# Bucket sums of both batches behind the second scores, and first products that wait for each part of their input

## The reference

```python
def causal_linear_attn(q, k, v):
    q = jax.nn.softmax(q, axis=-1)
    k = jax.nn.elu(k) + 1.0
    bq, bk, bv = (z.reshape(b, h, u, BUCKET, e) for z in (q, k, v))   # BUCKET 64, 4 buckets of 256 tokens
    k_cum = jnp.cumsum(bk.sum(axis=-2), axis=-2)
    ctx = jnp.einsum('bhund,bhune->bhude', bk, bv)
    ctx = jnp.cumsum(ctx, axis=2)
    ctx = ctx / (k_cum[..., None] + 1e-06)
    ctx = jnp.pad(ctx, ((0, 0), (0, 0), (1, 0), (0, 0), (0, 0)))[:, :, :-1]
    return jnp.einsum('bhund,bhude->bhune', bq, ctx)
...
for i in range(DEPTH):                                                # DEPTH 4
    x = x + self_attention(layer_norm(x, ln1_g[i], ln1_b[i]), Wq[i], Wk[i], Wv[i], Wo[i], bo[i])
    h = layer_norm(x, ln2_g[i], ln2_b[i])
    x = x + (jax.nn.gelu(h @ W1[i] + b1[i], approximate=False) @ W2[i] + b2[i])
```

## Time and profile before

| | |
|---|---|
| median of 3 runs | 1082.23 us (1082.07 to 1083.27) |
| the profiled execution | 1085.59 us, span 1083.8 us |
| busy in the span | PE 1000.8 us, PEld 845.2, DVE 680.7, ACT 560.8, POOL 483.0 |
| one step in the middle (409.92 to 456.79) | 46.87 us |

### The profile page before, as it was taken

The page is one execution under the profiler, slowest core; times in us unless marked ns, Lnnn a source line. Parts: engine busy times, 40 slices in busy tenths (PEclk is TensorE's granted clock), DMA queues, the critical chain, the costliest instruction groups (busy, mean ns, idle before and its releaser), DMA issues.

```text
span 1083.8 us, 22544 instructions
## 1 busy us (share of the span) xinstructions
PE 1000.8 (92%) x8461; PEld 845.2 (78%) x8461; DVE 680.7 (63%) x1502; ACT 560.8 (52%) x1338; POOL 483.0 (45%) x378
## 2 busy tenths in 40 slices
PE   3577999999999999999999999999999979999997
PEld 3455888888878878886887888788888758987887
DVE  2556576666857676776767667676341776657543
ACT  1416665756656574765657476665715333435210
POOL 7215446526843652585365358633416220006441
PEclk9777999999999999999999999999999999999999
DMA  5201000000300000021000102001036464640001
GB/s 186 79 1 39 2 2 16 2 16 2 98 24 2 16 2 16 2 79 42 2 15 2 16 2 79 2 2 45 2 95 165 123 157 98 143 112 1 20 20 40
DMA packets 71547, 47.72 MB, mean 44 GB/s; under 512 B 44463, under 2 KB 68111, under 8 KB 71439
## 3 DMA queue, kind: packets, MB, share of 16 engines
q1 hardware_dynamic: 71439, 46.27, 15.6%
HBM read 44.16 MB, written 2.10 MB: 43 GB/s over the span
## 4 chain that ended last, share of the span: by engine, by line
PE 65%; DVE 10%; ACT 8%; SPq 7%; issue 6%; POOL 2%; DMA 1%; POOLq 0%; DVEq 0%; ACTq 0%
PE A L1099 17%; PE F L1099 16%; PE F L1220 13%; ACT prob L920 5%; PE A L1465 4%; PE A L1130 3%; SPq L298 2%; PE A L1169 2%; DVE smax L582 2%; DVE xt L519 2%; PE A L1186 2%; PE A L1125 2%; SPq L306 1%; SPq L308 1%; PE A L1438 1%
## 5 line engine op out<-in xcount | busy, mean ns | idle before, releaser
L1099 PE MATMUL F<-xt,w 128*128 128x512 f32 x960 | 244.5, 405 | 8.3 <-ACT scratch L1082 3.9
L1099 PEld LDWEIGHTS F<-xt,w 128*128 128x128 f32 x960 | 176.1, 190 | 56.2 <-DVE xt L519 7.7
L385 POOL TENSOR_TENSOR ht<-scratch,ht 128x512 fp32r<-128x512 f32 x128 | 175.0, 1386 | 46.0 <-ACT ht L952 44.9
L1220 PEld LDWEIGHTS F<-w,ht 128*128 128x128 f32 x1536 | 182.8, 188 | 11.8 <-issue 9.3
L1220 PE MATMUL F<-w,ht 128*128 128x256 f32 x1536 | 189.3, 282 | 1.9 <-POOL ht L385 1.9
L374 POOL TENSOR_TENSOR rstd<-var,minus_half 128x4 f32<-128x4 f32 x32 | 38.0, 1187 | 242.5 <-DVE var L501 242.5
L949 ACT ACTIVATE scratch<-F,b_now 128x512 f32<-128x512 f32 x128 | 87.6, 685 | 43.1 <-PE F L1099 22.1
L1099 PE MATMUL A<-wa,xt 128*128 128x512 f32 x384 | 96.5, 409 | 3.8 <-issue 3.6
L1099 PEld LDWEIGHTS A<-wa,xt 128*128 128x128 f32 x384 | 74.2, 196 | 21.6 <-issue 3.9
L380 POOL TENSOR_TENSOR x<-x,vec_f 128x1024 f32<-128x1024 f32 x16 | 37.9, 2368 | 105.5 <-DVE scratch L514 105.5
L952 ACT ACTIVATE ht<-scratch 128x512 fp32r<-128x512 f32 x128 | 80.9, 632 | 4.1
(11 more groups left out here) (200 smaller groups left out, 1960.2 us busy)
## 6 DMA issues: line engine op xcount, KB each, us to landing
raw_f<-in_L_attn_W_dram SPq DMA_DIRECT2D x8, 1024.0 KB, 5.5
scratch<-in_L_ffn_fc_B_dram SPq DMA_DIRECT2D x32, 256.0 KB, 3.5
scratch<-in_L_ffn_fc_A_dram SPq DMA_DIRECT2D x32, 256.0 KB, 3.5
x<-in_x_dram SPq DMA_DIRECT2D x4, 512.0 KB, 7.4
raw_f<-in_L_ffn_fc_A_dram SPq DMA_DIRECT2D x32, 64.0 KB, 2.3
scratch<-in_x_dram SPq DMA_DIRECT2D x1, 2048.0 KB, 9.4
raw_f<-in_L_ffn_fc_B_dram SPq DMA_DIRECT2D x32, 64.0 KB, 3.0
out_dram<-x SPq DMA_DIRECT2D x3, 512.0 KB, 2.9
```

Source lines behind the costliest of these rows:

```text
L385: pool.tensor_tensor(ht[:, 1, m, :], hf[:, m % 2, :], ht[:, 0, m, :].bitcast(F32), ALU.subtract).then_inc(h_lo, 1)
L1099: last = pe.matmul(out, lhs(a, c), rhs(b, c), start=k == 0, stop=k == len(total) - 1)
L1220: last = pe.matmul(F[:, t % 2, 0:D], ht[:, a, c, P * t:P * t + P], w2[:, b, c, :], start=k == 0, stop=k == len(passes) - 1)
```

## The change

Three things change. `pe_ctx` makes the sums of both batches in one go, in banks 0 and 1 for batches 0 and 1, with the 128-token pieces of both batches first; it stands behind `pe_s(1)` and in front of `y(3)`. The wait for ACT's copy of the query transposes (`qnt_out`) moves from `pe_s(1)` to the sums. `dve_ctx` handles both batches with one set of three operations, behind the minimum of the second batch. And a new `first_product`, used by `pe_h(0)` and `pe_qk(0)`, waits for the low half of chunk 0, then for the high half of chunk 1 in front of the fourth matmul, and for the low half of chunk 1 in front of the sixth.

```diff
-        def dve_ctx(dve, n, b):
+        def dve_ctx(dve, n):
...
-            dve.wait_ge(ctx_psum, 2 * n + b + 1)
-            ps = A[:, 1 - b, 0:3 * HB].rearrange("p (j e) -> p j e", j=3)
-            dve.tensor_scalar(kcum[:, b, :], ps[:, :, E], 1e-6, None, ALU.add).then_inc(kcum_done, 1)
+            dve.wait_ge(ctx_psum, n + 1)
+            ps = A[:, 0:2, 0:3 * HB].rearrange("p b (j e) -> p b j e", j=3)
+            dve.tensor_scalar(kcum[:, :, :], ps[:, :, :, E], 1e-6, None, ALU.add).then_inc(kcum_done, 1)
...
                 if attn:
-                    dve_ctx(dve, n, 0)
                     dve_max(dve, n, 1)
+                    dve_ctx(dve, n)
                 y_add(3)
                 if attn:
-                    dve_ctx(dve, n, 1)
                     dve_prec(dve, n)
...
+        def first_product(pe, out, lhs, rhs, i, n):
+
+            total = [(c, a, b) for c in range(DC) for a, b in PASSES]
+            for k, (c, a, b) in enumerate(total):
+                if k == 0:
+                    pe.wait_ge(xt_lo[i], 2 * n + 1)
+                elif (a, b) == (0, 0):
+                    pe.wait_ge(xt_hi[i], 2 * n + c + 1)
+                elif b == 1 and c == 1:
+                    pe.wait_ge(xt_lo[i], 2 * n + c + 1)
+                last = pe.matmul(out, lhs(a, c), rhs(b, c), start=k == 0, stop=k == len(total) - 1)
+            return last
...
             if i == 0:
-                pe.wait_ge(xt_lo[0], 2 * n + 2)
                 pe.wait_ge(wa_ready, l + 1)
+                first_product(pe, A[:, QK_BANKS[i], :], lambda a, c: wa[:, a, c, P * i:P * i + P],
+                              lambda b, c: xt[0][:, b, c, :], 0, n).then_inc(qk_psum, 1)
+                return
...
                 pe.wait_ge(exp_done, 2 * n + 1)
-                pe.wait_ge(qnt_out, n + 1)
...
-        def pe_ctx(pe, n, b):
-
-            def part(j, t, rows, start, stop):
+        def pe_ctx(pe, n):
+
+            def part(b, j, t, rows, start, stop):
                 for h in range(NH):
-                    last = pe.matmul(A[E * h:E * h + E, 1 - b, j * HB:(j + 1) * HB], kexp[0:rows, t, E * h:E * h + E],
+                    last = pe.matmul(A[E * h:E * h + E, b, j * HB:(j + 1) * HB], kexp[0:rows, t, E * h:E * h + E],
                                      v8[0:rows, t, NH + h, :], start=start, stop=stop, skip_group_check=True)
                 return last
-            part(0, 2 * b, BUCKET, True, False)
-            part(2, 2 * b + 1, BUCKET, False, False)
-            part(2, 2 * b, P, False, False)
-            part(1, 2 * b, P, False, True).then_inc(ctx_psum, 1)
+            for b in range(2):
+                part(b, 2, 2 * b, P, True, False)
+                part(b, 1, 2 * b, P, False, False)
+            for b in range(2):
+                part(b, 0, 2 * b, BUCKET, False, False)
+                last = part(b, 2, 2 * b + 1, BUCKET, False, True)
+            last.then_inc(ctx_psum, 1)
...
                     pe_qnt(pe, n)
-                    pe_ctx(pe, n, 0)
                     pe_s(pe, n, 1)
+                    pe.wait_ge(qnt_out, n + 1)
+                    pe_ctx(pe, n)
                     y(3)
-                    pe_ctx(pe, n, 1)
```

More of the change, by code:

```diff
@@ L556, in dve_features2 @@
                               ALU.mult).then_inc(qn_done, 1)
-        def dve_ctx(dve, n, b):
-            dve.wait_ge(ctx_psum, 2 * n + b + 1)
-            ps = A[:, 1 - b, 0:3 * HB].rearrange("p (j e) -> p j e", j=3)
-            dve.tensor_scalar(kcum[:, b, :], ps[:, :, E], 1e-6, None, ALU.add).then_inc(kcum_done, 1)
[L563 to L567, removed]
+        def dve_ctx(dve, n):
+            dve.wait_ge(ctx_psum, n + 1)
+            ps = A[:, 0:2, 0:3 * HB].rearrange("p b (j e) -> p b j e", j=3)
+            dve.tensor_scalar(kcum[:, :, :], ps[:, :, :, E], 1e-6, None, ALU.add).then_inc(kcum_done, 1)
+            dve.wait_ge(kcum_done, n + 1)
+            dve.reciprocal(kcum[:, :, :], kcum[:, :, :]).then_inc(krec_done, 1)
+            dve.wait_ge(krec_done, n + 1)
+            dve.tensor_tensor(ctxn[:, :, :, 0:E], ps[:, :, :, 0:E],
+                              kcum[:, :, :].rearrange("p b (j o) -> p b j o", o=1).broadcast_to([P, 2, 3, E]),
                               ALU.mult).then_inc(ctxn_done, 1)
@@ L1090, in pe_xt @@
                     if lin is not None and c == DC - 1 and t == TILES - 1:
-                        pe.wait_ge(ctxn_done, 2 * lin + 2)
+                        pe.wait_ge(ctxn_done, lin + 1)
                     last = pe.transpose(xt_bank(i, c)[:, P * t:P * t + P], xh[i][:, t, P * c:P * c + P], ident[:, :])
@@ L1202, in pe_h @@
             if m == 0:
-                pe.wait_ge(xt_lo[1], 2 * n + 2)
                 pe.wait_ge(w1_ready, l + 1)
+                first_product(pe, F[:, 0, :], lambda a, c: w1[:, a, c, 0:P],
+                              lambda b, c: xt[1][:, b, c, :], 1, n).then_inc(h_psum, 1)
+                return
             if m >= 2:
@@ L1369, in step @@
                     if not mlp:
-                        pe.wait_ge(ctxn_done, 2 * n + 2)
+                        pe.wait_ge(ctxn_done, n + 1)
                     pe_lin(pe, n)
```

## The result

The changed kernel takes **1065.25 us** (median of 4 runs, 1062.58 to 1066.43), the kernel before 1082.15 us (4 runs, 1081.75 to 1083.27): a ratio of 0.9839, 95% interval 0.9817 to 0.9861. The profiled executions are 1085.59 us before and 1066.43 us after, their spans 1083.8 and 1064.4.

The account below looks back on a forecast made before the run. PE's own order, busy 92% of the span, was taken as the bound. Gains of 3.9 (order), 1.7 (first two steps) and 4.1 us (waits by part) sum to 9.7: 1082.2 - 9.7 = 1072.5 us, range 1067.5 to 1079.5.

Parts of the forecast that it names:

- the two stalls: PE idle 0.43 us before the first MLP product, for DVE's low half, and 0.26 us before the second scores, for ACT's copy.
- the stall of 0.43 us: PE before the first MLP product: removed by earlier scores, net 0.28 us in each of 14 steps, 3.9 us.
- what speaks against the change: Before the MLP transposes, waiting for L614 covered the second batch's sums; moved, their 0.59 us are no longer free.
- T = 1.00: PE's cost in us for all 64 rows of sums in one block, put between 1.00 and 1.70.
- the transposes at 0.53: PE's query transposes, taken to last 0.53 us as before, with the second scores now following them.
- 0.15 us later: MLP input transposes on PE come 6.53 us behind the query transposes, against 6.38 before.
- 25 ns a row: Trainium skill's floor for small matmuls: the block of sums would take 1.6 us, total about 1081; chance 0.03.
- the query product at 0.10: Waiting part by part before the query product removes 3.00 - 2.90 = 0.10 us in eleven steps.
- the steps with the split of W1 and W2: Three steps where POOL splits W1 and W2: the query product's waits by part save 0.57 us each.
- the second rival: PE stalls as long at the next place, or late stages take the gain back; 1077 to 1080, chance 0.16.
- the clock as a width only: Low granted clock after the loop's jump back: a shift gives back 1.6 us or brings it twice, on every case.
- 1.7 + 0.65 + 0.1: First two steps' earlier score chain, 1.7 us; very first step's product wait, 0.65; a query product's wait, 0.10.

Follow-up runs that it names:

- only the order: Changed kernel, with the first MLP product and first query product again waiting for their whole input; 1072.27 us, ratio 0.9895 to the kernel before.
- only the waits: Kernel before, with the first MLP product and first query product waiting for each part of their input; 1068.97 us, ratio 0.9873.
- Both fastest kernels: Changed kernel with the sums behind the output's last quarter, 1059.89 us; changed kernel with the MLP transposes' wait for DVE's adds split by bank, 1059.57 us.

## Why the prediction was right or wrong

**Right: what bounds the kernel, and the two stalls.** The scores moved up, the chain to the low half with them, and the stall of 0.43 us went, with the waits part by part as a spare for it. The kernels with only the order, with only the waits, and with the MLP product's waits taken back show each of these. The merging of DVE's small operations had no run of its own, but the add L614 starts 3.16 us behind the start of the quarter, where it was 3.13, so it delayed nothing. (The prediction said that this add isn't due before 431.9; by its own rows it would be 431.52 + 0.15 = 431.67. Nothing hung on it.)

**Right: what speaks against the change.** The sums of the second batch had been covered by the wait for L614, and it stayed 3.64 us from the quarter to the transposes (3.61 before). Both fastest kernels live off this gap.

**Wrong in size: T = 1.00 and the transposes at 0.53.** This is the step of the prediction that failed, the cost of PE's path from the query transposes to the last quarter: it was to get longer, and it got shorter. The block took 0.77 us and the query transposes, now followed by a product of the same shape, 0.43. Instead of 0.15 us later, the input's transposes come 232.23 - 225.99 = 6.24 us behind the query transposes, 0.14 us earlier than the 6.38 of the earlier trace rows. The prediction had also weighed 25 ns a row for the block; it took 12. This is 0.3 us a step, and the largest term that was off: in the ten regular steps of 2 to 14 and the last one 11 x 0.3 = 3.3 us.

**Wrong in size: the query product at 0.10.** It cost 0.22 (the kernel with only the order, against the changed one): I read the time between starts in front of the product and not the slower first matmuls behind the stall, because I compared with a product that had a stall of its own in front. 10 x 0.12 = 1.2 us.

**Half right: the steps with the split of W1 and W2.** Here 0.28 + 0.57 = 0.85 us each were forecast. They took 49.19, 49.12 and 47.30 us between the starts of their token products, where before it was 50.15, 49.85 and 48.05: 0.96, 0.73 and 0.75. Of the 0.96, 0.34 are the idle time at the loop's first jump, 1.57 us and not 1.91, and in the second profile of the changed kernel it was 2.00. The query product's wait went as forecast (3.47 to 2.89), but as much came up again, in front of the product of probabilities and values:

```profile
285.87 3.04 PE L1098 MATMUL F<-xt,w 128*128 128x512 f32 x12
289.69 1.51 PE L1202 MATMUL A<-scratch 128*32 128x256 f32 x32 [0.78 <-DVE scratch L587]
```

Before, the idle time in that place was 0.20 us:

```profile
297.73 1.51 PE L1186 MATMUL A<-scratch 128*32 128x256 f32 x32 [0.20 <-DVE scratch L587]
```
This is what the second rival had said of these steps; why DVE is later there was not tested.

**Wrong: the clock as a width only.** I allowed 1.6 us either way, behind the jump. The trace shows two places. Behind the first jump 24 matmuls took 7.26 us before and 5.71 after. In step 1 the transposes of the probabilities and the first MLP products, 24 matmul rows, ran in part at the low level of 1.2 GHz in the kernel before, and at the high level of 2.4 GHz after; windows of the kernel before and of the changed one (granted clock third from the end):

```profile
99.52:105.32 5.80, 5.80 (x25) 5.11 (x26) 5.49 (x18) 3.58 (x7) 3.33 (x4) 0.71 0.29 75
```

```profile
96.06:100.23 4.17, 4.17 (x24) 3.59 (x25) 3.93 (x9) 3.57 (x7) 3.98 (x4) 1.00 0.00 0
```

5.80 against 4.17 us: 1.6 us again. Both places look so in both profiles of each kernel (step 1 in the second ones: 5.78 us at 0.70, and 4.17 at 1.00). Whether every timed run of the kernel before has them isn't shown: the timed run beside its second profile took 1083.21 us at a mean clock of 0.982, the profile 1084.72 at 0.979.

**The account**, between the spans 1083.8 and 1064.4, 19.4 us. Up to the start of step 2, 123.70 - 118.41 = 5.3 us, forecast 1.7 + 0.65 + 0.1 = 2.45; of the 2.85 that lack, 1.6 are step 1's clock. Another 0.75 lie in front of step 0 (its token products start at 23.67 us before and 22.92 after), where nothing was changed, and the second profiles have 24.25 and 24.29 there: this part is scatter. The rest was not followed further. Steps 2 to 14, 12.85 us, forecast 6.3; of the 6.5, 10 x 0.5 = 5.0 are regular steps and 1.55 is the jump. From the start of step 15 on, 1.3, forecast 0.9. So T, the changes of shape and the query product (3.3 + 1.2 us) make about half of the miss of 9.7 us between the profiles, the clock (1.6 + 1.55) a third. Between the medians of the timed runs the gain is 16.9 us and the miss 7.2; how much of the clock's part is in it isn't shown.

**The range** held T up to 1.15 and the clock by 1.6 us, but below the forecast it had only "a little under 1.00" for T. The lower bound was worked out from batches that change their rows inside and end in a change of shape, and was not a lower bound.

## What to carry to other kernels

The cheapest thing to try is to cut a semaphore wait for a whole input into parts: here it gave 14 us alone, and where it wasn't needed it cost nothing that could be measured. When small products of several array shapes stand in one block, sort them by shape before pricing them, and price them by such a sorted run. And look at what a moved block had covered: the place it left stayed as long as it was, and putting the block there, or letting half of the next work in, gave 5.4 and 5.7 us more.

## What the runs showed of the hardware

A change of a matmul's rows from 128 to 64 or back costs 0.14 us on PE (64 rows of sums: 0.77 us with one change, 1.18 with four). The Trainium skill says in TensorEngine Tiling (Array Packing), Key Properties, that changing the tiling mode drains the engine; this trace agrees as far as it shows it, with 0.12 to 0.13 us between the starts on both sides of each change and no more than 0.03 inside a piece.

A stall of PE can cost more than its idle time: the twelve rows of the query and the key product take 2.90 us behind a stall and 2.80 without. The MLP product gains less by it, 2.90 to 2.88: behind the transposes its first two starts are 0.31 us apart even where nothing stalls, and 0.34 behind the stall.

The granted clock behind the first jump of the loop was 0.76 in both profiles of the kernel before, and 1.00 in both of the changed one. The kernel with only the order had the drop too (24 matmuls in 7.25 us), the other experiments had not. The length of PE's idle time in front does not sort them: it was 1.91 and 1.85 us in the two profiles of the kernel before and 2.00 with only the order, where the clock dropped, and 1.57 and 2.00 in the two profiles of the changed kernel, where it did not. What decides it was not settled.
